# Bidirectional gate sums from one scan over another, computed two tiles at a time and spread as single instructions over four stages

## The reference, cut to what matters

```python
ek, euk = exp(min(k, 30)), exp(min(u + k, 30))
# forward: a_t = a_(t-1) * decay + ek_t * v_t      b_t = b_(t-1) * decay + ek_t
# backward: the same, from the last token to the first
num = nf + nb - ek * v + euk * v
den = df + db - ek + euk
gate = sigmoid(r) * (num / max(den, 1e-8)) * (0.8 + 0.2 * tf)
x = x + sub_block(x_gated)
```

## Time and profile before

| | us |
|---|---|
| median of 3 runs | 2892.4 |
| lowest, highest | 2892.08, 2892.63 |
| the profiled execution, its own time | 2891.36 |
| its span, first to last instruction | 2889.6 |
| mean granted TensorE clock | 0.912 of full |

### The profile page before, as it was taken

How to read it: one execution, slowest core, us unless ns; L and a number is a source line. 1 busy time by engine, 2 the same in 40 slices (tenths; PEclk the granted TensorE clock), 3 DMA queues, 4 the chain that set the end, 5 groups by cost and what they waited for, 6 DMA issues and landing times.

```text
span 2889.6 us, 33412 instructions
## 1 busy us (share of the span) xinstructions
PE 2286.2 (79%) x10127; PEld 1699.1 (59%) x10144; DVE 2056.9 (71%) x2931; ACT 912.7 (32%) x1891; POOL 719.7 (25%) x566
## 2 busy tenths in 40 slices
PE   0567868868768379988946887898889988899998
PEld 0234334334334167866735666787777767688887
DVE  8889889889889755666655556666666666666665
ACT  2123223223223223233313333334433434322222
POOL 2234334244235223434431102212211221000000
PEclk9988989989889789999977889999989998999999
DMA  4001001001002423243241100000000100100001
GB/s 176 15 22 37 22 15 41 17 18 40 15 22 76 151 88 109 69 145 135 68 157 41 30 18 29 22 11 33 22 7 29 44 22 22 51 22 22 32 12 59
DMA packets 51464, 141.93 MB, mean 49 GB/s; under 512 B 5760, under 2 KB 5760, under 8 KB 47056
## 3 DMA queue, kind: packets, MB, share of 16 engines
q1 hardware_dynamic: 32192, 91.72, 9.2%
q10 hardware_dynamic: 13536, 30.97, 3.0%
q0 software_dynamic: 5680, 18.62, 2.1%
HBM read 106.95 MB, written 34.34 MB: 49 GB/s over the span
## 4 chain that ended last, share of the span: by engine, by line
issue 49%; PE 21%; POOL 12%; POOLq 9%; DVE 5%; ACT 2%; DMA 1%; DVEq 0%; ACTq 0%; SPq 0%
PE bank L328 6%; PE bank L329 6%; PE bank L330 6%; POOLq L453 3%; POOLq L466 3%; POOLq L463 3%; POOL g_v L454 2%; POOL g_e L462 2%; POOL g_eu L464 2%; POOL g_v L470 2%; PE bank L1861 1%; POOL aw_lo L414 1%; POOLq L681 1%; POOL ug L682 1%; DVE rinv L1566 1%
## 5 line engine op out<-in xcount | busy, mean ns | idle before, releaser
L1761 PE MATMUL bank<-um,w_in 128*128 128x512 f32 x576 | 282.2, 643 | 70.8 <-DVE state L1260 26.0
L1761 PEld LDWEIGHTS bank<-um,w_in 128*128 128x128 f32 x576 | 114.1, 206 | 216.9 <-issue 127.1
L973 ACT ACTIVATE probs<-bank,nmx 128x128 f32<-128x128 f32 (+3 forms) x256 | 131.6, 527 | 178.9 <-DVE nmx L1569 178.9
L328 PE MATMUL bank<-u_hi,aw_hi 128*128 (+1 forms) x384 | 160.4, 418 | 9.4 <-issue 9.4
L328 PE MATMUL bank<-pt_hi,v_hi 128*128 128x512 f32 (+3 forms) x256 | 91.7, 358 | 92.9 <-DVE pt_lo L1584 90.1
L448 DVE RECIPROCAL g_ek<-g_eu 128x512 f32<-128x512 f32 x47 | 157.6, 3353 | 1.6
L461 POOL TENSOR_TENSOR g_ek<-g_ek,g_r 128x511 f32<-128x511 f32 x47 | 66.4, 1414 | 368.8 <-DVE g_ek L440 368.8
L1584 DVE TENSOR_TENSOR pt_lo<-bank,pt_hi 128x512 fp32r<-128x512 f32 (+1 forms) x192 | 109.2, 596 | 67.9 <-ACT pt_hi L980 67.9
L329 PE MATMUL bank<-u_lo,aw_hi 128*128 (+1 forms) x384 | 152.8, 398 | 0.0
L330 PE MATMUL bank<-u_hi,aw_lo 128*128 (+1 forms) x384 | 152.2, 396 | 0.0
L980 ACT ACTIVATE pt_hi<-bank 128x512 fp32r<-128x512 f32 (+1 forms) x192 | 94.0, 526 | 146.7 <-PE bank L1861 146.7
(11 more groups left out here) (351 smaller groups left out, 6431.4 us busy)
## 6 DMA issues: line engine op xcount, KB each, us to landing
m_stage<-in_moe SPq DMA_DIRECT2D x24, 1024.0 KB, 6.0
y_slot<-m_o ACTq DMA_DIRECT2D x39, 256.0 KB, 3.3
g_v<-in_fT SPq DMA_DIRECT2D x34, 256.0 KB, 2.6
gates<-g_v SPq DMA_DIRECT2D x33, 256.0 KB, 2.0
f_stage<-in_ffn SPq DMA_DIRECT2D x11, 768.0 KB, 4.3
u_g<-gates SPq DMA_DIRECT2D x8, 1024.0 KB, 5.7
gates<-g_v ACTq DMA_DIRECT2D x27, 256.0 KB, 2.0
g_v<-in_fT ACTq DMA_DIRECT2D x26, 256.0 KB, 3.0
```

What stands on the lines that cost most here:

```text
L328: nc.tensor.matmul(out, hi_w, hi_x, start=start, stop=False)
L973: A(probs[:, h % 2, PR_AT[qb]:PR_AT[qb] + w], S_[bk][:, c0:c0 + w], ACT.Exp, bias=nmx[:, h % 2, qb:qb + 1], scale=SCALE, accum_out=rsum[:, ...
L1761: mm = M(dst[:], w_in[:, k, c0:c0 + P], um[:, k, :], start=(k == 0), stop=(k == KC - 1))
```

## The change

**Mathematics.** The backward scan now runs over the result of the forward scan, in place. With weights of an infinite sequence that gives the two-sided sum divided by 1 - d^2, so ek is multiplied by `inflow` = 1 - d^2 in its clamp, and the last column of each forward sum is multiplied by `edge` = 1 / (1 - d^2) before the backward scan (128x2 elements, L468). The own token is counted once, as `- ek` asks. Still four scans a tile, all of 512 columns, and no arrays r1, r2. POOL has two additions a tile instead of four. decay is held below 1 by a clamp, and `inflow` and `edge` cost five small instructions in setup.

**Two by two.** 30 pairs of tiles. DVE writes both denominators to the places of the sums (`gate_dens`), POOL multiplies them, DVE takes one reciprocal of the product (`gate_inverse`, 128x512), and POOL gets both quotients from it with four multiplications (`gate_result`). A pair has 13 POOL instructions, where two tiles had 14. A buffer `g_v` holds two pairs; the exponentials of the next pair wait for the sums and for the first result of the pair before (`gate_exps`), since all pairs of a stage share `g_s` and `g_eu`.

**Where.** Setup and mamba: still 34 tiles, now pairs 0 to 16. Experts: 14 tiles (before 13), a pair for six blocks, the seventh in the last three blocks. Attention: 12 tiles (before 13), none in iteration 2, a pair for two iterations from 3 to 14. The attention loop of ACT and DVE is written out for four iterations, without branches, and the pieces are cut to single scans and to reciprocals of 256 columns, each put at another place of the iteration.

**Beside it.** PE's wait for `dt_abs` becomes two waits for `ob_read`, DVE's reads of bank 0 and 1. Some buffers share memory (`txm` in `lm`, `tx_moe` in `xdt`, `rms_inv` in `e2`), expert outputs have two buffers instead of three, and some semaphores are merged.

```diff
+        def gate_clamp(eng, k, s, t):
+            _, _, ek, eu = g_tile(s, t)
+            eng.wait_ge(g_exp, k * 4 + (2 * t + 2))
+            nc.vector.tensor_scalar(ek, ek, EXP30, inflow[:, bass.ds(k * 2 + (G_VEC + t), 1)], ALU.min, ALU.mult).then_inc(g_clamped, 1)
+            nc.vector.tensor_scalar(eu, eu, EXP30, None, ALU.min).then_inc(g_clamped, 1)
+        def gate_forward(eng, k, s, t, i):
+            x = g_tile(s, t)[1 + i]
+            if i == 0:
+                eng.wait_ge(g_pool, k * P_PAIR + P_PRODUCTS[t])
+            d = decay[:, bass.ds(k * 2 + (G_VEC + t), 1)].to_broadcast([P, T])
+            nc.vector.tensor_tensor_scan(x, d, x, 0.0, ALU.mult, ALU.add).then_inc(g_vec, 1)
+        def gate_backward(eng, k, s, t, i):
+            x = g_tile(s, t)[1 + i]
+            if i == 0:
+                eng.wait_ge(g_vec, k * V_PAIR + V_EDGE[t])
...
+            nc.vector.tensor_tensor_scan(x[:, ::-1], d, x[:, ::-1], 0.0, ALU.mult, ALU.add).then_inc(g_vec, 1)
+        def gate_inverse(eng, k, s, half=None):
+            r = g_tile(s, 1)[2]
+            eng.wait_ge(g_pool, k * P_PAIR + P_DENS)
+            if half is None:
+                nc.vector.reciprocal(r, r).then_inc(g_vec, 2)
+            else:
+                o = slice(half * (T // 2), (half + 1) * (T // 2))
+                nc.vector.reciprocal(r[:, o], r[:, o]).then_inc(g_vec, 1)
+        def gate_result(eng, k, s):
+            (v0, d0, _, _), (v1, d1, r, _) = g_tile(s, 0), g_tile(s, 1)
...
+            eng.wait_ge(g_vec, k * V_PAIR + V_PAIR)
+            mult(d1, r, d1, ALU.mult)
+            mult(d0, r, d0, ALU.mult)
             eng.drain()
+            mult(v0, v0, d1, ALU.mult).then_inc(g_pool, 1)
+            mult(v1, v1, d0, ALU.mult).then_inc(g_pool, 1)
...
+            def pair_gate(k, s):
+                for t in range(2):
+                    gate_products(pool, k, s, t)
+                for t in range(2):
+                    gate_add(pool, k, s, t)
+                gate_den_product(pool, k, s)
+                gate_result(pool, k, s)
```

DVE in mamba, token blocks:

```diff
-                    gate(mamba_tile(b, 2 if tb else 1), tb - 1 if tb else 2)
+                    if tb == 0:
+                        inverse(mamba_pair(b, 0))
+                        clamp(mamba_pair(b, 1), 0)
+                    elif tb == 1:
+                        scans(mamba_pair(b, 1), 0)
+                        clamp(mamba_pair(b, 1), 1)
+                    elif tb == 2:
+                        scans(mamba_pair(b, 1), 1)
+                    else:
+                        dens(mamba_pair(b, 1))
```

DVE in mamba, head pairs j:

```diff
-                    if j % 2 == 0:
-                        gate(mamba_tile(b, 3 + j // 2), 1)
+                    if j == 0:
+                        clamp(third, 0)
+                    elif j == 1:
+                        scans(third, 0)
+                        clamp(third, 1)
+                    elif j == 2:
+                        scans(third, 1)
+                    elif j == 3:
+                        dens(third)
+                    elif j == 4:
+                        inverse(third)
+                    elif j == 5:
+                        clamp(fourth, 0)
+                    elif j == 6:
+                        scans(fourth, 0)
+                        clamp(fourth, 1)
                     else:
-                        gate(mamba_tile(b, 3 + j // 2), 2)
-                        gate(mamba_tile(b, 4 + j // 2), 0)
-                gate(mamba_tile(b, 7), 1)
+                        scans(fourth, 1)
```

DVE in the experts, after the work of block (h, q):

```diff
+                if (h, q) == (0, 0):
+                    scans((k, s), 0)
+                elif (h, q) == (0, 1):
+                    scans((k, s), 1)
+                elif (h, q) == (0, 2):
+                    inverse((k, s))
+                elif (h, q) == (1, 2):
+                    clamp((k + 1, s), 0)
+                    clamp((k + 1, s), 1)
```

DVE in attention, where g == 0 is the first half of a pair (iterations 3, 5, ...) and g == 1 the second:

```diff
                 ctx_lo(i, 1)
+                if g == 0:
+                    gate_forward(dve, *pair, 0, 0)
+                elif g == 1:
+                    gate_inverse(dve, *pair, 0)
                 pt_lo_split(i, 2, (0, 1))
...
                 pt_lo_split(i, 3, (0, 1))
-                with_gate(lambda: gate_scans(dve, n, a_ek[:], a_e[:], a_r1[:], a_r2[:]))
                 if not last:
                     row_max(i + 1, 0)
                 pt_lo_split(i, 3, (2,))
+                if g == 0:
+                    gate_backward(dve, *pair, 0, 0)
+                    gate_backward(dve, *pair, 0, 1)
```

PE at the start of a sequence:

```diff
-                pe.wait_ge(dt_abs, b + 1)
                 for q, ch in enumerate(CONV_ORDER):
                     if q >= 2:
                         pe.wait_ge(conv_tapped, N_CONV * b + q - 1)
+                    else:
+                        pe.wait_ge(ob_read, KC * b + (q + 1))
```

More of the change, by code:

```diff
@@ L994, in _, with att_act @@
             att_hi(1, 1)
-            def att_act(i, first, last):
+            def att_act(i, mod, u=None):
+                first, last = mod == "first", mod == "last"
+                half, k = (0, 1, 0, 1)[mod - 3] if u is not None else None, None
+                if u is not None:
+                    k = u * 2 + (G_ATT + (mod - 3) // 2)
                 vt_copy(i)
@@ L1017, in att_act @@
                 ctx_hi(i, 1)
-                if not (first or last):
-                    with act.If(i >= A_GATE):
-                        g_load(act, n, A_SLOT, use)
                 pt_hi_copy(i, 2)
@@ L1151, in _ @@
                 setup.inc(V.tensor_tensor(um[:, i, :], pre_v[i], pre_ek[i], ALU.mult))
-                for slot, part in (((0, 0),), ((0, 1),), ((0, 2), (1, 0)), ((1, 1),))[i]:
-                    gate((G_VEC + slot, slot, 0), part)
+                if i == 0:
+                    clamp((0, 0), 0)
+                elif i == 1:
+                    scans((0, 0), 0)
+                    clamp((0, 0), 1)
+                elif i == 2:
+                    scans((0, 0), 1)
+                else:
+                    dens((0, 0))
             setup.wait()
```

580 lines of the change are left out of this document (326 added, 254 removed).

## The result

The changed kernel takes 2773.5 us (median of 4 runs, 2771.9 to 2779.0); the kernel before took 2892.2 us beside it. The ratio is 0.959, with a 95% interval of 0.958 to 0.960: 119 us less, where the prediction said 134. The profiled execution is the longest of the four (2778.95 us, span 2777.2, granted clock 0.921).

The account below looks back on a forecast made before the run. PE, with its waits for DVE, bounds attention and experts; a chain through DVE mostly bounds mamba. Attention -94, mamba -38, experts -1 and setup -1 sum to -134 us from 2892.4, giving 2758 us, range 2715 to 2815.

Parts of the forecast that it names:

- Attention, -109 + 15 = -94: Attention: 82.4 us of PE waits for pt_lo and the half clock behind them go, 109 us, less 15 us charged.
- The half clock: Attention: PE's granted clock of 0.50 after long waits for pt_lo goes with those waits, 27 us gained.
- The charge of 15 us: Attention: 1.25 us lost in each of 12 iterations, since the new places have no spare time; bounds 0 and 45.
- Head and last tail, -9 a sequence and -8: Mamba: earlier first chunk and shorter convolution gate parts, 9 us gained a sequence; last sequence's norm reciprocal earlier, 8 us.
- Token blocks, +8.5 a sequence: Mamba token blocks: more DVE gate work and a new 4 us wait for POOL, 8.5 us lost, bounds 5 and 11.
- Head pairs, -8.5 a sequence: Mamba head pairs 0 to 6: half of 16 us less DVE gate work counts, 8.5 us gained, bounds 4 and 13.
- 6 us for slow scans: Mamba: 6 us kept back for scans that POOL makes slower, turning -44 into -38.
- Experts, setup: Experts, PE-bound: -1 us, bounds -10 and +12; setup: one reciprocal part less against small added instructions, -1 us.
- 1 (pieces still hold PE): Attention: single pieces still hold PE up, each iteration keeping 2.5 us and a half clock, +35 us, 2793; chance 0.15.
- 2: Mamba gives nothing, the new POOL wait and PE's work eating it, 2796; chance 0.08, shared with a combined case of 2831.
- 3 (slow scans): Mamba and attention: every gate scan takes 1.06 us more beside POOL, 2939; chance 0.05 in full.
- 4: The change does not free the place: single pieces wait for POOL as the scans did, +50 us, 2808; chance 0.05.

Follow-up runs that it names:

- e7: Kernel before, with only attention's four scans of a tile moved to two other places (behind pt_lo(i, 3, (2,)) and ctx_lo(i, 3)): 2809.9 us, ratio 0.9718.
- e2: Changed kernel with every VectorE gate instruction of the pairs on 8 columns instead of 512: 2635.3 us.
- e8: Kernel before, with GpSimd's additions and result multiplication of every gate tile on 8 columns instead of 512: 2781.5 us.
- e4: Changed kernel, but PE waits for dt_abs again ahead of the convolution's first projection: 2781.4 us, ratio 0.9614.
- e9: Changed kernel with mamba's first-pair reciprocal behind the convolution's last taps, and some attention scans and the second half reciprocal moved: 2748.6 us, ratio 0.9504.
- e3: Changed kernel with GpSimd's additions, product of denominators and four result multiplications of every pair on 8 columns instead of 512: 2686.8 us.
- e5: Changed kernel, but in setup and mamba VectorE makes each of a sequence's four reciprocals twice: 2828.2 us, ratio 0.9775.

## Why the prediction was right, and where it was not

- **The bound.** Right for attention: e7 shows that the scans behind pt_lo held PE, and that the place alone is worth 83 us. For the head pairs "DVE sets the pace" was half the truth. It was read from 70.5 busy us of 71.2. But with almost no gates on VectorE (e2) they still take 58.2 us, with VectorE busy for 34 of them, and part of the 70.5 was instructions that took longer beside GpSimd, which the profile counts as busy: narrowing GpSimd alone takes 11.2 us from this window (e8).
- **Attention, -109 + 15 = -94.** The 82.4 us of stalls went: 9.0 us are left in that row. The half clock gave 22.7 us, not 27. New is 15 us of waits for the probabilities, 1.49 us in most iterations. The charge of 15 us was the right size, and its reason (GpSimd's additions beside `normalise`) is what the rows show. The clock in attention is 0.95 and not over 0.97; between 1748 and 2287 us it is 1.00. Iterations take 49.2 to 53.5 us from 5 to 12, 56.5 to 57.1 in 3, 13 and 14.
- **Head and last tail, -9 a sequence and -8.** From the gating of pair 6 to the first xdt of the next sequence took 102.7, 101.0 and 101.1 us before and 90.9, 91.0 and 91.3 after, so 10 to 12 us less, where 9 were forecast. The first sequence gained 5.2 us up to there, for 9: PE's wait for dt was only 3.06 us in it. The last tail gained 6.4, for 8. In all 43 us in place of 44. The path was right too: PE ends the output product 34.1 us after the gating of pair 6, and before it was 34.0 in the mean, so the gate work saved in the tail gave PE nothing there; what went is PE's wait behind the dt products, and 3 us of the convolution. Where the reason was off is the changed wait: it alone is worth 2 to 3 us a sequence (e4), and VectorE's earlier output reads the rest.
- **Token blocks, +8.5 a sequence.** Measured +39 us in four up to the last state sum, 34 were forecast; the way from there to the masked product of pair 1 took 0.7 us more in four, so it was free, as said. The new wait for GpSimd is 3.59 us, 4 were forecast, and e9 takes it away.
- **Head pairs, -8.5 a sequence.** This is the term that was mis-sized: -5.3, so -20.5 us in four and not -34. These 13.5 us are as much as mamba fell short, since the 5 us by which the token blocks were dearer come out of the 6 us kept back for slow scans. VectorE's busy time in the window fell from 70.5 to 53.1 us, by 17.4, as counted (16). I took half of it as gain, and a third came. e3 and e8 put 3.8 of the 5.3 us down to GpSimd, which the term didn't have; VectorE's own saved work gave the other 1.5 (60.0 against 58.5 us with GpSimd narrow). That the term came out within its bounds owes something to luck.
- **6 us for slow scans.** Measured 9.8 us in mamba (1360 against 1208 ns, 64 times). But masked product, gating and other instructions pay more, 48 us together in the changed kernel. I saw the mechanism only in the scans. It was there before the change too, so it did not move the sum by that much.
- **Experts, setup.** -2.7 and -3.1 us, for -1 and -1. The +4.2 us behind `v_lo` of iteration 15 was not foreseen. PE is at half clock there for 13.7 us of the last iteration, 6.8 before; but e9, with 6.8 us again, has 419.9 us for this stretch (416.5 before), so this explains little of it, and the cause stays open.
- **The rivals.** 1 (pieces still hold PE) fell as priced. The 9.0 us of waits for pt_lo that are left stay with VectorE's gate instructions on 8 columns (e2: 9.2 us), so no piece causes them. What the pieces cost attention with GpSimd's work that they release is the 15 us at `normalise`, which the sum had; attention came out 5 us above the forecast. 2 fell: mamba gave 24 us. 3 (slow scans) fell: the mean is 1.31 and not 2.28 us. The rule that was named for it (the Trainium skill, GPSIMD Engine Reference, Specifications) holds for more instructions than I applied it to. 4 fell in attention (no piece waits there for GpSimd) and is true in one place of mamba.

## What to carry to other kernels

Look first at where a helper's instructions stand, then at how many there are: a free slot is between an engine's last contribution to the critical ring and its next, and e7 had 70% of the whole gain from moving four scans. In mamba the number counted too: with two reciprocals for a pair (e5) the stage is slower than before the change. Before a stage is called bound by VectorE, ask how many of its busy microseconds are instructions that take longer than their own best row. Place GpSimd's work, by placing what releases it, beside VectorE instructions that read PSUM.

## What the runs showed of the hardware

Sorted by whether GpSimd ran beside them for over 90% of their time, the instructions of the changed kernel's trace fall in two classes:

| VectorE instruction, 512 columns | alone, us | beside GpSimd, us |
|---|---|---|
| scan, two operands in SBUF (L463) | 1.21 | 2.29 |
| lm x cb, two operands in SBUF (L1413) | 0.69 | 1.53 |
| gating xa x tz, two in SBUF (L1431) | 0.69 | 1.64 |
| denominator, one in SBUF and a column (L491) | 0.48 | 1.15 |
| xdt, PSUM and a factor in SBUF (L1390) | 0.68 | 0.68 |
| state sum, PSUM and SBUF (L1371) | 0.69 | 0.69 |
| row maximum from PSUM (L1713, longest) | 0.68 | 0.68 |

The values are means; "beside" rests on 4, 20, 4, 7, 20, 12 and 6 instructions, from the first row to the last. GpSimd pays as well: one of its additions beside two scans took 2.18 us (L516 at 692.5 us) and 1.27 alone.

The whole reciprocal, one operand in SBUF, kept 3.34 us where GpSimd worked during a part of it (6 of 24). A backward scan never had GpSimd beside it. That an instruction with an operand in PSUM is not held, where its twin in SBUF takes twice as long, is what I had not used. The Trainium skill, SBUF — State Buffer, section Who interferes with whom, has both classes, copies and tensor_scalar among the ones that can be held; by that rule, this trace agrees in every row of the table. It also says that whichever comes second is blocked until the other's whole instruction is over. The rows here show instructions that take 0.7 to 1.1 us more beside GpSimd ones of 1.3 us, which fits a wait for the end of one, but no row shows which started first.

The half clock followed a PE wait of 4.48 us at head 3 and did not follow one of 1.68 us at head 0.
